# Per-batch attention matrices built from 64-row heads in place of block-diagonal pairs, in a flamingo block on Trainium2

## What is computed

```python
x = x + tanh(g_xattn) * xattn(layernorm(x), ctx, ctx, w_q, w_k, w_v, w_o)   # this stage is changed
x = x + tanh(g_ffn) * ffn(layernorm(x), w_gate, w_up, w_down)               # quantised FFN, not touched

# xattn, 16 heads of 64, 4 batches, 1024 queries and 64 keys for each batch
q = heads(query @ w_q); k = heads(ctx @ w_k); v = heads(ctx @ w_v)
scores  = einsum('bhqd,bhkd->bhqk', q, k) * 64**-0.5   + causal mask (only the first 128 queries see it)
weights = softmax(scores)
out     = einsum('bhqk,bhkd->bhqd', weights, v) -> (b, 1024, 1024) @ w_o
```

## Time and profile before

| what | value |
|---|---|
| runs | 1479.95, 1481.16, 1481.19 us; median 1481.16 |
| profiled execution, own time | 1489.47 us |
| its span | 1487.7 us |
| TensorE's mean granted clock | 0.952 of full speed |
| front phase | about 0 to 560 us of the span |
| busy: PE / DVE / ACT / POOL | 89% / 70% / 43% / 17% |

### The profile page before, as it was taken

How to read it: one execution, slowest core, us unless ns; L and a number is a source line. 1 busy time by engine, 2 the same in 40 slices (tenths; PEclk the granted TensorE clock), 3 DMA queues, 4 the chain that set the end, 5 groups by cost and what they waited for, 6 DMA issues and landing times. The chain is left out here.

```text
span 1487.7 us, 18885 instructions
## 1 busy us (share of the span) xinstructions
PE 1329.8 (89%) x6142; PEld 1090.9 (73%) x6142; DVE 1034.5 (70%) x1397; ACT 644.7 (43%) x769; POOL 259.7 (17%) x312
## 2 busy tenths in 40 slices
PE   7899999999999978999999999999992019999999
PEld 6778777777877856888888778877882018888887
DVE  0379669767966655777777679999998984545453
ACT  3334334333333214333334255556667973333331
POOL 1024224213412220001000035541020000000000
PEclk9999999999999998999999999999996559999999
DMA  8003212312322435766664889986558963444543
GB/s 311 1 22 114 79 43 92 99 42 71 102 75 82 171 112 204 247 238 238 247 240 157 272 295 308 317 312 208 174 197 335 318 228 116 161 166 151 175 144 118
DMA packets 111248, 259.77 MB, mean 175 GB/s; under 512 B 10832, under 2 KB 23120, under 8 KB 109648
## 3 DMA queue, kind: packets, MB, share of 16 engines
q1 hardware_dynamic: 110896, 259.04, 50.2%
q10 hardware_dynamic: 288, 0.00, 0.0%
HBM read 152.04 MB, written 106.95 MB: 174 GB/s over the span
## 5 line engine op out<-in xcount | busy, mean ns | idle before, releaser
L1097 PE MATMUL gpG<-xph,Wh 128*128 128x512 f32 x384 | 153.2, 399 | 6.0 <-DVE xpl L1021 6.0
L1571 PE MATMUL pD<-Wh,xph 128*128 128x512 f32 x384 | 150.5, 392 | 4.6 <-DVE xpl L1550 4.6
L1097 PE MATMUL pU<-xph,Wh 128*128 128x512 f32 x384 | 150.6, 392 | 2.2 <-ACT ust L1222 1.2
L1097 PE MATMUL gpG<-xph,Wl 128*128 128x512 f32 x384 | 150.8, 393 | 0.0
L1097 PE MATMUL gpG<-xpl,Wh 128*128 128x512 f32 x384 | 150.7, 392 | 0.0
L1097 PE MATMUL pU<-xpl,Wh 128*128 128x512 f32 x384 | 150.3, 391 | 0.0
L1571 PE MATMUL pD<-Wh,xpl 128*128 128x512 f32 x384 | 150.3, 391 | 0.0
L1097 PE MATMUL pU<-xph,Wl 128*128 128x512 f32 x384 | 150.2, 391 | 0.0
L1571 PE MATMUL pD<-Wl,xph 128*128 128x512 f32 x384 | 150.2, 391 | 0.0
L1550 DVE TENSOR_TENSOR xpl<-doq,xph 128x1536 fp32r<-128x1536 int16 (+1 forms) x34 | 56.4, 1663 | 122.4 <-ACT xph L1517 122.4
L1004 ACT ACTIVATE gst<-gpG,sc 128x512 f32<-128x512 f32 x96 | 66.3, 691 | 168.8 <-PE gpG L1097 168.8
(11 more groups left out here) (172 smaller groups left out, 2884.0 us busy)
## 6 DMA issues: line engine op xcount, KB each, us to landing
dub<-up_d SPq DMA_DIRECT2D x42, 768.0 KB, 4.7
gate_d<-gst SPq DMA_DIRECT2D x96, 256.0 KB, 2.3
gb<-gate_d SPq DMA_DIRECT2D x32, 768.0 KB, 6.0
up_d<-ust SPq DMA_DIRECT2D x96, 256.0 KB, 4.1
xr<-xn_d SPq DMA_DIRECT2D x9, 1024.0 KB, 6.0
xph<-up_d SPq DMA_DIRECT2D x11, 768.0 KB, 6.3
xpl<-up_d SPq DMA_DIRECT2D x11, 768.0 KB, 6.2
xin<-in_x SPq DMA_DIRECT2D x32, 256.0 KB, 2.6
```

The lines of the kernel that those rows point to most:

```text
L1097: mm = pe.matmul(ps[:, :], Ws[:, it, kt * P:(kt + 1) * P], xs[:, kt, :], start=(kt == 0 and Ws is Wh and xs is xh), stop=(kt == KT - 1 and ...
L1571: mm = pe.matmul(pD[4 * t + q][:, :], os_[n][:, cs], Ws[:, it, :], start=(it == 0 and os_ is oh and Ws is Wh), stop=(it == IT - 1 and os_ ...
```

## The change

- `diagonal`, kbd, vbd and their zeroing are gone. `of_batch` copies the keys (or values) of a batch to kb (vb), 128 x 8 x 64, in one ScalarE instruction of 128 rows.
- A and V are made in four **units** for each matrix in place of eight chunks. A unit fills two banks, even heads in one and odd heads in the other: heads are 64 rows of the array each, an even head in rows 0 to 63, an odd one in rows 64 to 127.
- A unit of A: 8 pairs x 2 heads = 16 float32 matmuls, 64 rows, 128 stationary columns, 64 moving columns. A unit of V: 4 matmuls, 64 rows, 64 stationary columns, 512 moving columns; the two pairs of a unit go to output partitions 0 to 63 and 64 to 127, so each matmul uses a quarter of the array.
- Units alternate between pT and pS[0], with a wait for the low parts of the unit before last. A unit follows every second pair of the values.
- The columns of A, and so the scores and softmax weights, are now ordered even heads first. V's row blocks follow: block 4a+u holds heads 4u+a and 4u+2+a. In a V step the values take the pairs in the order 0, 4, 1, 5, 2, 6, 3, 7.
- New or moved waits on TensorE: before a matrix's first unit, for `scores_down` of tile k-2+which (its pS bank must be free); scores of the tile k % 8 = 0 wait for the first six low parts of A; scores of the tile k % 8 = 2 wait for all low parts of V; the transposes before them wait for all but the last two. `apart_e` is a semaphore increment on TensorE ahead of each unit.

```diff
-def diagonal(act, t, bd, b, done):
-    for a in range(2):
-        rows = slice(a * 64, a * 64 + 64)
-        act.activation(bd[rows, :, a * 64:a * 64 + 64], t[rows, :, bass.ds(CK * b, CK)], ACT.Copy).then_inc(done, 1)
+def of_batch(act, t, tb, b, done):
+    act.activation(tb[:, :, :], t[:, :, bass.ds(CK * b, CK)], ACT.Copy).then_inc(done, 1)
...
+        def unit_banks(k, which, u):
+            return pT if u % 2 != which else pS[(k + which) % 2]
...
-            pool.memset(kbd[:, :, :], 0.0).then_inc(bd_zero, 1)
-            pool.memset(vbd[:, :, :], 0.0).then_inc(bd_zero, 1)
...
-            def chunk(b, ahead, which, n):
-                pe.wait_ge(*at(ch_lo, NCH * b, NCH * ahead + 8 * which + n - 1))
-                bank = pT[:, (n % 2) * 512:(n % 2 + 1) * 512]
+            def unit(b, k, ahead, which, u):
+                banks = unit_banks(k, which, u)
+                pe.wait_ge(*at(ch_lo, NCH * b, NCH * ahead + 8 * which + max(2 * u - 2, 0)))
                 if which == 0:
-                    for q in range(4):
-                        pair = (n % 2) * 4 + q
-                        mm = pe.matmul(bank[:, q * P:(q + 1) * P], wqT[:, pair, (n // 2) * P:(n // 2 + 1) * P],
-                                       kbd[:, pair, :], start=True, stop=True)
+                    pe.sem_inc(apart_e, 1)
+                    for pair in range(PAIRS):
+                        for a in range(2):
+                            rows = slice(a * HD, a * HD + HD)
+                            mm = pe.matmul(banks[:, a * 512 + pair * CK:a * 512 + (pair + 1) * CK],
+                                           wqT[rows, pair, u * P:(u + 1) * P], kb[rows, pair, :], start=True, stop=True)
+                            if pair == PAIRS - 1:
+                                mm.then_inc(ch_ps, 1)
                 else:
-                    mm = pe.matmul(bank, vbd[:, n, :], wo[:, n, :], start=True, stop=True)
-                mm.then_inc(ch_ps, 1)
+                    pe.sem_inc(apart_e, 1)
+                    for c in range(2):
+                        for a in range(2):
+                            rows = slice(a * HD, a * HD + HD)
+                            mm = pe.matmul(banks[c * CK:(c + 1) * CK, halves[a]], vb[rows, 2 * u + c, :], wo[rows, 2 * u + c, :],
+                                           start=True, stop=True)
+                            if c == 1:
+                                mm.then_inc(ch_ps, 1)
...
-                for p in range(PAIRS):
+                for i in range(PAIRS):
+                    p = i % 2 * 4 + i // 2 if which == 1 else i
...
-                    if which is not None:
-                        if p == 1 and have(j):
+                    if which is not None and i % 2 == 1:
+                        if i == 1:
+                            pe.wait_ge(*tile(sub_done, b, k - 2 + which))
+                        if i == 3 and have(j):
                             pe.wait_ge(*part(pTl_done, b, j, 1))
-                        chunk(b, ahead, which, p)
+                        unit(b, k, ahead, which, i // 2)
...
             def scores(b, k):
+                if k % BQ == 2:
+                    pe.wait_ge(*at(ch_lo, NCH * b, NCH * (k // BQ) + NCH))
                 for kt in range(KT):
                     if k % BQ == 0:
-                        pe.wait_ge(*at(ch_lo, NCH * b, NCH * (k // BQ) + 2 * kt + 2))
+                        pe.wait_ge(*at(ch_lo, NCH * b, NCH * (k // BQ) + max(2 * kt + 2, 6)))
...
-                        if k % BQ == 2 and p % 4 == 0:
-                            pe.wait_ge(*at(ch_lo, NCH * b, NCH * (k // BQ) + NCH - 1 + p // 4))
+                        if k % BQ == 2 and p == 0:
+                            pe.wait_ge(*at(ch_lo, NCH * b, NCH * (k // BQ) + NCH - 2))
```

More of the change, by code:

```diff
@@ L151, in flamingo_block @@
                 with ExitStack() as early:
-                    kbd = sb(early, "kbd", [P, PAIRS, P], F32)
-                    vbd = sb(early, "vbd", [P, PAIRS, P], F32)
+                    kb = sb(early, "kb", [P, PAIRS, CK], F32)
+                    vb = sb(early, "vb", [P, PAIRS, CK], F32)
                 xr = [sb(rows, f"xr{n}", [P, 4, H], F32) for n in range(2)]
@@ L157, in flamingo_block @@
                 pX = [pb(rows, f"gpX{n}") for n in range(KT)]
-                front_phase(mk, xf, cf, (w_q, w_k, w_v, w_o), (wqT, wo, kT, vT, kbd, vbd, wk, wv, Ah, Al), g_xattn, g_ffn, w_src[0], wsc[0],
+                front_phase(mk, xf, cf, (w_q, w_k, w_v, w_o), (wqT, wo, kT, vT, kb, vb, wk, wv, Ah, Al), g_xattn, g_ffn, w_src[0], wsc[0],
                             load_w[0], xr, xr_in, pS, pX, x1_d, xn_d, ident, mask, half, xmx,
@@ L319, in front_phase @@
     w_q, w_k, w_v, w_o = weights
-    wqT, wo, kT, vT, kbd, vbd, wk, wv, Ah, Al = shared
+    wqT, wo, kT, vT, kb, vb, wk, wv, Ah, Al = shared
     TG_X, TG_F, RAW_X, RAW_F, S_X, INV_X, T0, T1 = cols
@@ L368, in front_phase @@
         pT_ps, pTh_done, pTl_done = (sem(n, 16) for n in ("pT_ps", "pTh", "pTl"))
[L370 to L371 removed]
+        kb_set, vb_set = sem("kb_set"), sem("vb_set")
+        apart_p, apart_e = sem("apart_p"), sem("apart_e")
         masked, apart, sx_red, sx_spread, sx_scale = (sem(n) for n in ("masked", "apart", "sx_red", "sx_spread", "sx_scale"))
@@ L538, in step @@
                 if k == 5 and have(BQ):
-                    diagonal(act, kT, kbd, b + 1, kbd_set)
-                    diagonal(act, vT, vbd, b + 1, vbd_set)
+                    of_batch(act, kT, kb, b + 1, kb_set)
+                    of_batch(act, vT, vb, b + 1, vb_set)
                 if have(k - 2):
@@ L583, in step @@
                     act.wait_ge(*at(ch_ps, NCH * b, NCH * ahead + 8 * which + n + 1))
+                    bank = unit_banks(k, which, n // 2)[:, halves[n % 2]]
                     if which == 0:
-                        act.activation(Ah[:, n // 2, (n % 2) * 512:(n % 2 + 1) * 512], pT[:, (n % 2) * 512:(n % 2 + 1) * 512],
-                                       ACT.Copy, scale=SCALE).then_inc(ch_hi, 1)
+                        act.activation(Ah[:, n // 2, halves[n % 2]], bank, ACT.Copy, scale=SCALE).then_inc(ch_hi, 1)
                     else:
-                        act.activation(Vh[:, n, :], pT[:, (n % 2) * 512:(n % 2 + 1) * 512], ACT.Copy).then_inc(ch_hi, 1)
+                        act.activation(Vh[:, n % 2 * 4 + n // 2, :], bank, ACT.Copy).then_inc(ch_hi, 1)
                 if which == 0:
@@ L605, in _ @@
                     copied(wqT[:, 2 * r + a:2 * r + a + 1, :], pw[a], wqT_ps, 2 * r + a + 1, wqT_sb)
-            act.wait_ge(bd_zero, 2)
             act.wait_ge(k_sb, ROUNDS)
-            diagonal(act, kT, kbd, 0, kbd_set)
+            of_batch(act, kT, kb, 0, kb_set)
             for r in range(ROUNDS):
@@ L615, in _ @@
             act.wait_ge(v_sb, ROUNDS)
-            diagonal(act, vT, vbd, 0, vbd_set)
+            of_batch(act, vT, vb, 0, vb_set)
             schedule(act, step)
@@ L620, in _, with chunk_low @@
         def _(dve):
-            def chunk_low(b, ahead, which, n):
+            def chunk_low(b, k, ahead, which, n):
                 dve.wait_ge(*at(ch_hi, NCH * b, NCH * ahead + 8 * which + n + 1))
-                bank = pT[:, (n % 2) * 512:(n % 2 + 1) * 512]
+                bank = unit_banks(k, which, n // 2)[:, halves[n % 2]]
                 if which == 0:
-                    cs = slice((n % 2) * 512, (n % 2 + 1) * 512)
+                    cs = halves[n % 2]
                     dve.scalar_tensor_tensor(out=Al[:, n // 2, cs], in0=bank, scalar=SCALE, in1=Ah[:, n // 2, cs].bitcast(F32),
@@ L628, in chunk_low @@
                 else:
-                    dve.tensor_tensor(Vl[:, n, :], bank, Vh[:, n, :].bitcast(F32), ALU.subtract).then_inc(ch_lo, 1)
+                    q = n % 2 * 4 + n // 2
+                    dve.tensor_tensor(Vl[:, q, :], bank, Vh[:, q, :].bitcast(F32), ALU.subtract).then_inc(ch_lo, 1)
             def scores_down(b, j):
@@ L685, in step @@
                 which, ahead = matrices(k, have)
-                chunks = [lambda n=n: chunk_low(b, ahead, which, n) for n in range(8)] if which is not None else []
+                chunks = [lambda n=n: chunk_low(b, k, ahead, which, n) for n in range(8)] if which is not None else []
                 def some(n):
```

19 lines of the change are left out of this document (9 added, 10 removed).

## The result

The changed kernel took 1492.28 us (median of 5 runs, 1487.88 to 1493.33), the kernel before 1481.19 (median of 5 runs, 1479.95 to 1486.07). The ratio is 1.0056, 95% interval 1.0035 to 1.0078: 8 us slower by the ratio, 11 by the medians. The forecast was 1486 in a range of 1456 to 1516, slower with a chance of 0.52. The total came out near the forecast; its parts did not.

A forecast was written before the change was run, and what follows sets the result against it. TensorE's order of work was taken to bound the kernel. Later A steps +1.9, later V steps +7.2, batch 0's A -4.8 and V +0.5 make +4.8 us on the median 1481.16: 1486 us, range 1456 to 1516.

The forecast's parts named there:

- What bounds it: Whole kernel: TensorE, busy 89% of the span, sets the time by its order of work; shifts carry to what follows.
- A's matmuls: Units of A: loads of different row halves run side by side, 1.62 us of streaming, 1.96 with change-over against 1.80.
- V's matmuls: Units of V: eight records take 2.15 us, between 0.87 and 3.46; unit 2.49 against 1.73, +2.4 a later step.
- the rival with full overlap: Units of A and V: halves and quarters all run side by side; together -24, 1457 us; chance 0.15.
- Between the shapes: Around each unit: changing the array from whole to divided and back costs 0.17 us each time, 0.34 a unit.
- Later A steps: Three later A steps: four units cost 0.16 us more each, +0.64 a step, +1.9 us in all.
- TensorE's clock drops from 2.4 to 1.2 GHz in the units: Units: a condition named as making the forecast wrong; given no size and no chance.
- Waits: Later steps: new waits for scores_down and A's six low parts cost nothing; about 1.2 us for V's last low part.
- Batch 0: First batch: A's scores start 4.8 us earlier, including 0.63 from one ScalarE copy fewer; V costs +0.5 us.
- The sum: Whole kernel: 1.9 + 7.2 - 4.8 + 0.5 = +4.8 us, added to the median 1481.16, giving 1486.
- quarters overlap, A does not gain: Units: A as forecast, V's quarters all side by side; -14 us, 1467; chance 0.15.
- the full overlap of both: Same as the rival with full overlap: units of A and V, -24 us, 1457; chance 0.15.

The follow-up runs named there:

- a_full: Changed kernel with A's matmuls on all 128 rows, block-diagonal keys, 64 moving columns each; 1514.78 us in one run.
- a_quarters: Changed kernel, A's stationary columns cut to 64 (quarters of the array): 1465.84 us; a_quarters_warm adds 14 useless matmuls before later A steps: 1461.05 us.
- warm: Changed kernel plus 14 useless matmuls (the filling) in TensorE's wait ahead of each later A step; 1478.57 us, ratio 0.9969 to the kernel before.
- before_warm: Kernel before with the same 14 useless matmuls ahead of each later A step; 1481.22 us against 1482.57, ratio 0.9990.

## Why the prediction was right, and where not

- **What bounds it**: right. TensorE's order carried the gains and losses of the steps through to the end of the front phase.
- **A's matmuls**, "loads of different halves run side by side, but a load still takes the time of 128 columns": right, and shown by a_full and a_quarters. Forecast 0.10 us a head, measured 0.11; a unit 2.14 us, forecast 1.96. The missing 0.18 lies in a reading of the earlier trace rows. A chunk's 0.90 us was split there into eight records of 0.10 and 0.09 by which the next matmul is late; the records start 0.111 apart, which gives 0.89 with nothing late. So two chunks stream 1.78, a unit of A as long, and the change of shape comes on top in full: +0.34 a unit, not +0.16.
- **V's matmuls**: the step that failed. "Each matmul's second record uses the same quarter as its first and must follow it. If starts keep the order of the program" gave 5 slots, 2.15 us. The runs show 2 slots, close to the 0.87 that was the bound from below: the first records of all four quarters start within 0.02 us of each other, so one quarter does not wait for the second record of another. The term was +2.4 us a V step; it measured -2.7, which is what the rival with full overlap gave for V.
- **Between the shapes**: 0.17 us a change was forecast. In the V step a unit costs 1.23 for 0.86 of streaming, so the two changes are 0.37 together, 0.19 each. The Trainium skill's sentence that a mode change drains TensorE (TensorEngine Tiling (Array Packing), "Key Properties") fits this, though no run shows the drain itself. For A the same comes out of a_full: 0.35 a unit with row halves, nothing on the whole array. It is no large cost.
- **Later A steps**: +0.64 us each was forecast. At 2.4 GHz throughout it is 26.38 (warm) against 25.01 (before_warm), +1.4, of which 4 x (2.14 - 1.80) = 1.36 is the unit's cost. The traced steps lost 1.3, 5.0 and 6.0, the rest being the clock. The prediction named "TensorE's clock drops from 2.4 to 1.2 GHz in the units" among what would make it wrong and gave it neither price nor chance. It should have: it stands in the kernel before, where the first chunk after the 3.48 us wait takes 1.91 us and not 1.05, and a change that alters what TensorE does right after a wait must be priced at both levels. In the later A steps the clock does not drop in the units; it is down before the first of them and rises late. In batch 0 it did drop in a unit (at 53.3 us), as the prediction had named it.
- **Waits**: no wait for scores_down before the first V unit and none for six low parts of A, as forecast; 1.00 us for the last low part of V (about 1.2).
- **Batch 0**: the 0.63 us of ScalarE shows as a wait of 2.21 before the second x transposes in place of 3.00. The scores after A were to start 4.8 us earlier and started 0.9 earlier (58.43 against 59.32): units 2 and 3 took about 2.4 more at or near 1.2 GHz, and the step itself began 0.6 later where 0.63 earlier was forecast. V was put at +0.5 and came at -2.2, in the main for the reason above.
- **The sum**: +1.9 + 7.2 - 4.8 + 0.5 was forecast. By the steps of the table it was +12.3 (later A), -8.1 (later V), +0.9 (A of batch 0) and -2.2 (V of batch 0). With the 0.6 by which batch 0's A begins later that is 3.5 us in the two traces. The forecast came near the total by luck: V was 18 us better than forecast (-10.3 against +7.7), A about 17 us worse (+10.4 in the later steps, +6.3 in batch 0 with its late start). Of the +10.4 the clock is 8.2: against the steps with the filling, the later steps of the changed kernel lost 14.0 us, those of the kernel before 5.8. Of the rivals, "quarters overlap, A does not gain" had the mechanism right, with 0.15, and missed the clock; the full overlap of both, 1457, is near what a_quarters_warm reaches (1461), with another cut of A and with the filling.

## What to carry to other kernels

Small float32 matmuls on parts of the array ran side by side here, but their weight loads paced them where 128 stationary columns met 64 moving ones: cut the array both ways, so that the stationary columns do not outnumber the moving ones. A stretch of load-paced matmuls behind a wait of 3.5 us stayed at 1.2 GHz for up to nearly 24 us here; price what follows each wait at both levels, or keep TensorE fed through the wait with work that has free operands and a free bank. Before one change with two parts is dropped as slower, time the parts: here one was worth -8.6 us, the other +21, and the second could be mended.

## What was not expected of the hardware

- Records of all four quarters of the array start together, and so do their loads: 8 records of 512 moving columns took 1.09 us from the first start to the last end, where one alone is 0.64 long, and 64 of 64 columns took 1.16. The two records of one float32 matmul did not hold back matmuls on other quarters.
- The pace of a record with 64 moving columns: 0.110 us on the whole array with 128 stationary columns, the same as with 128 moving ones (0.111), 0.056 on row halves, 0.015 on quarters with 64 stationary columns.
- TensorE was busy without a gap for 12.7 us at a granted clock of 0.51. By the Trainium skill (TensorE: Matmul & The Clock Gate, "Why this matters for your kernels"), keeping TensorE busy without gaps brings the fast clock. It did not in this stretch of half-array units and values, so the measurement differs from the page and decides. Why the level rises sooner with full-array chunks was not settled: they differ from the units in rows used and in moving columns, and a_full, with all rows and 64 moving columns, also ran units at half speed (7.04 us for 32 records in batch 0, and a granted clock of 0.50 from 304.5 to 318.0 in the A step of batch 2). Long half speed thus came without row halves too.
